# Moving the attention mask multiplication from VectorE to GpSimd and adding weight loads of the identity on TensorE

## What is computed

```python
q = k = v = src.reshape(B, S, H, 64).transpose(0, 2, 1, 3)
scores = q @ k.T                                # no scaling
valid  = (|k_pos - q_pos| <= 256) & inside the sequence
attn   = softmax(where(valid, scores, -1e9)) @ v
x  = layernorm(src + attn)
x  = layernorm(x + relu(x @ W1 + b1) @ W2 + b2)     # 1024 -> 4096 -> 1024
x  = layernorm(src + x)
x  = layernorm(x + moe(x))     # 8 experts, the top 2 weighted by a gate, silu(gate) * up
```

## Time and profile before

| | us |
|---|---|
| runs of the kernel | 3070.01 and 3357.81, median 3213.91 |
| the profiled execution | 3068.48, its span 3067.3 (cores 3056.1 to 3067.3) |
| attention | 481 of the span |
| TensorE busy, whole span | 2279.9 (74%) |
| VectorE busy, whole span | 942.5 (31%) |
| ScalarE busy, whole span | 507.6 (17%) |
| GpSimd busy, whole span | 147.5 (5%), issues of DMAs and four small fills at the start |

### The profile page before, as it was taken

The page is one execution under the profiler, slowest core; times in us unless marked ns, Lnnn a source line. Parts: engine busy times, 40 slices in busy tenths (PEclk is TensorE's granted clock), DMA queues, the critical chain, the costliest instruction groups (busy, mean ns, idle before and its releaser), DMA issues.

```text
span 3067.3 us, 30932 instructions; the slowest of 8 cores (3056.1 to 3067.3 us)
## 1 busy us (share of the span) xinstructions
PE 2279.9 (74%) x11113; PEld 1085.0 (35%) x11290; DVE 942.5 (31%) x1837; ACT 507.6 (17%) x750; POOL 147.5 (5%) x282
## 2 busy tenths in 40 slices
PE   0487777522998899303299988999899988999863
PEld 0244444311444344102144434444344443444431
DVE  0244455465000500554333311332123321233133
ACT  0233343200310220000011111111111111111110
POOL 2000000000000000000000010000100001000000
PEclk9999999999999899755599999999999999999987
DMA  9300000100443243030022233222332223322342
GB/s 220 73 1 1 1 1 1 42 0 0 72 79 69 48 78 67 14 110 0 21 35 42 42 62 58 40 43 47 58 60 35 43 48 62 55 42 38 52 97 75
DMA packets 49812, 148.14 MB, mean 48 GB/s; under 512 B 4936, under 2 KB 7664, under 8 KB 47616
## 3 DMA queue, kind: packets, MB, share of 16 engines
q0 software_dynamic: 39808, 115.49, 21.9%
q1 hardware_dynamic: 9856, 30.66, 3.3%
HBM read 248.96 MB, written 8.42 MB: 84 GB/s over the span
## 4 chain that ended last, share of the span: by engine, by line
PE 71%; DVE 12%; issue 5%; ACT 5%; DMA 4%; SPq 3%; DVEq 0%; ACTq 0%; POOL 0%; POOLq 0%
PE ob L652 14%; PE hg L587 14%; PE hu L587 14%; PE hb L467 7%; PE hb L438 7%; PE ps L331 5%; PE ppv L273 5%; DVE x0s L129 4%; DVE bn L129 3%; SPq L147 3%; ACT osb L139 2%; ACT strb L139 2%; DVE attnh L132 1%; PE ptm L293 1%; PE pbf L670 1%
## 5 line engine op out<-in xcount | busy, mean ns | idle before, releaser
L587 PE MATMUL hg<-ubf,w1T 128*128 128x512 bf16 x2007 | 482.9, 381 | 19.9 <-DMA w1T<-w1tt 10.1
L587 PE MATMUL hu<-ubf,w1T 128*128 128x512 bf16 x2007 | 479.9, 379 | 2.2
L652 PE MATMUL ob<-a,w2t 128*128 128x512 bf16 x1997 | 451.7, 381 | 17.3 <-DVE a L129 9.1
L129 DVE TENSOR_TENSOR x0s<-pbf,x0s 128x1024 f32<-128x1024 bf16 x80 | 97.9, 1224 | 928.2 <-PE pbf L670 493.6
L587 PEld LDWEIGHTS hg<-ubf,w1T 128*128 128x128 bf16 x2048 | 200.5, 98 | 261.6 <-issue 23.5
L129 DVE TENSOR_TENSOR sg<-sg,crep 128x512 bf16<-128x512 bf16 x256 | 108.8, 425 | 596.8 <-ACT sg L139 575.1
L587 PEld LDWEIGHTS hu<-ubf,w1T 128*128 128x128 bf16 x2048 | 200.5, 98 | 242.0 <-issue 0.7
L652 PEld LDWEIGHTS ob<-a,w2t 128*128 128x128 bf16 x2048 | 198.6, 98 | 246.0 <-issue 21.9
L139 ACT ACTIVATE sg<-hg 128x512 bf16<-128x512 f32 x256 | 152.9, 597 | 742.0 <-PE hu L587 742.0
L438 PE MATMUL hb<-ybf,w1buf 128*128 128x512 bf16 x1003 | 226.8, 386 | 14.7 <-ACT hsb L139 12.8
L139 ACT ACTIVATE strb<-ps 128x640 bf16<-128x640 f32 (+4 forms) x320 | 187.3, 597 | 288.4 <-PE ps L331 288.4
(11 more groups left out here) (64 smaller groups left out, 941.1 us busy)
## 6 DMA issues: line engine op xcount, KB each, us to landing
w1T<-w1tt POOLq DMA_DIRECT2D x64, 512.0 KB, 5.0
w2t<-w2tt POOLq DMA_DIRECT2D x128, 256.0 KB, 4.6
w1buf<-W1p POOLq DMA_DIRECT2D x32, 512.0 KB, 5.2
w2buf<-W2p POOLq DMA_DIRECT2D x16, 1024.0 KB, 9.0
x0s<-x SPq DMA_DIRECT2D x1, 8192.0 KB, 51.8
x0r<-x SPq DMA_DIRECT2D x1, 8192.0 KB, 28.1
out<-x0s SPq DMA_DIRECT2D x2, 4096.0 KB, 17.3
x0tm<-x0p POOLq DMA_DIRECT2D x20, 260.0 KB, 39.9
```

The source lines that it names most:

```text
L129: return self.vmark(getattr(self.nc.vector, name)(*args, **kw))
L587: ins = nc.tensor.matmul(hps[:], bass.AP(self.w1T, slot2 * 2048 + kc * 256 + hu * 128, [[2 * 2048, 128], [1, 128]]), self.ubf[:, kc, 512 * ...
L652: ins = nc.tensor.matmul(obp[:, 512 * nb:512 * nb + 512], self.w2t[:, dsl, eidx, 128 * jc:128 * jc + 128], self.a[:, eidx, jc, 1024 * half ...
```

## The change

The multiplication with the mask is issued on GpSimd in place of VectorE, with a semaphore of its own (`sGP`) that the products on TensorE, the reuse of the ring's slots by ScalarE, and the barriers wait for. Behind the scores of each strip one weight load of the 128x128 bf16 identity is issued on TensorE, and behind each group of five products two of them; no matmul uses these weights, since the next matmul is preceded by its own load. That is 320 + 2 x 256 = 832 weight loads more on a core.

```diff
--- before.py
+++ after.py
@@ -79,6 +79,8 @@
         self.sT = sem("sT")
         self.sV = sem("sV")
         self.sS = sem("sS")
+        self.sGP = sem("sGP")
+        self.cGP = 0
         self.NGL = 20
         self.NQL = 8
         self.gsems = [sem(f"g{i}") for i in range(self.NGL)]
@@ -138,6 +140,11 @@
     def sop_nw(self, name, *args, **kw):
         return self.smark(getattr(self.nc.scalar, name)(*args, **kw))
 
+    def gop_nw(self, name, *args, **kw):
+        self.cGP += 1
+        getattr(self.nc.gpsimd, name)(*args, **kw).then_inc(self.sGP, 1)
+        return self.cGP
+
     def qdma(self, out, in_):
         i = self.qrr
         self.qrr = (self.qrr + 1) % self.NQL
@@ -180,6 +187,7 @@
             self.wait(e, self.sT, self.cT)
             self.wait(e, self.sV, self.cV)
             self.wait(e, self.sS, self.cS)
+            self.wait(e, self.sGP, self.cGP)
             for i in range(self.NQL):
                 self.wait(e, self.qsems[i], self.qcnt[i])
             for i in range(self.NGL):
@@ -262,7 +270,7 @@
             grp = T // 4
             tloc = T % 4
             gb = h * 4 + grp
-            self.wait("tensor", self.sV, mask_mark[h * KT + T + 4])
+            self.wait("tensor", self.sGP, mask_mark[h * KT + T + 4])
             ppv = self.ppv[grp % 2]
             if tloc == 0:
                 self.wait("tensor", self.sV, evac_mark.get(gb - 2, 0))
@@ -275,6 +283,8 @@
                     self.x0tm[:, mm, 65 * h:65 * h + 65],
                     self.strb[:, sl, qc:qc + 128],
                     start=(i == 0), stop=(i == 4))
+            nc.tensor.ldweights(self.idb[:])
+            nc.tensor.ldweights(self.idb[:])
             pv_mark[gb] = pvm = self.tmark(ins)
             for mm in range(T, T + 5):
                 k = h * KT + mm
@@ -334,16 +344,18 @@
                         start=True, stop=True)
                     c0 += n
                 qk_m = self.tmark(ins)
+                nc.tensor.ldweights(self.idb[:])
                 self.wait("scalar", self.sT, qk_m)
                 if gidx >= RING:
                     self.wait("scalar", self.sT, strip_last_pv.get(gidx - RING, 0))
+                    self.wait("scalar", self.sGP, mask_mark.get(gidx - RING, 0))
                 exp_mark[gidx] = self.sop_nw(
                     "activation", self.strb[:, slot, 0:w], ps[:, 0:w],
                     AF.Exp, bias=-SHIFT, scale=1.0)
-                self.wait("vector", self.sS, exp_mark[gidx])
+                self.wait("gpsimd", self.sS, exp_mark[gidx])
                 if gidx >= RING:
-                    self.wait("vector", self.sT, strip_last_pv.get(gidx - RING, 0))
-                mask_mark[gidx] = self.vop_nw(
+                    self.wait("gpsimd", self.sT, strip_last_pv.get(gidx - RING, 0))
+                mask_mark[gidx] = self.gop_nw(
                     "tensor_mul", self.strb[:, slot, 0:w],
                     self.strb[:, slot, 0:w], self.msk[:, m, 0:w])
                 T = m - LAG
```

## The result

| | before | after |
|---|---|---|
| median of all runs (12 and 13) | 3107.43 us | 3111.56 us |
| ratio, after to before | | 1.007, 95% interval 1.0043 to 1.0097 |
| the profiled execution, its span | 3067.3 us | 3088.7 us |
| attention, every core | 481.7 us (481.4 to 481.8) | 497.2 us |

The account below looks back on a forecast made before the run. The prediction took TensorE in the attention, at 1.2 GHz and waiting for the copy at turns, as the bound. A head's +2.1 - 1.48 + 0.76 = +1.4 us gave +22 us on 3068.5, so 3090 us, range 3025 to 3140.

Parts of the forecast that it names:

- the sum: Attention, per head: +2.1 - 1.48 + 0.76 = +1.4 us; over 16 heads +22 us, attention 503 us.
- the same: Whole kernel: a change within about 2% (61 us), which a measurement cannot tell from no change; chance 0.72.
- In the other groups the mask hides behind TensorE: Groups after a head's first: GpSimd's masks cost nothing there, up to a price of about 1.6 us.
- The three steps behind the first products: Start of a head: products wait for masks 1.53 us apart instead of 1.31, 3 x 0.22 = 0.66 us more.
- Part 1: Turns inside a head: without the mask ahead on VectorE, the copy to attnh starts earlier, gaining 1.48 us a head.
- Part 2: GpSimd: a mask of 640 columns costs 1.53 us, 2.4 ns a column all in; bounds 0.77 and 2.06 us.
- Where the price lies: Start of a head: first products 1.44 us later, 2.1 us in all to the first turn; otherwise hidden behind TensorE.
- Part 3: TensorE in attention: 832 weight loads at 0.027 us each, 0.081 us a strip where TensorE sets the pace, 0.76 us a head.
- GpSimd setting the pace: Attention: a full strip's mask of 1.8 us or more makes GpSimd the bound, +62 us, from 3131 us; chance 0.17.
- Nothing moves: Attention: a cheap mask under 1.2 us with the clock unchanged gives 3045 to 3070 us; chance 0.05.
- The clock: TensorE in attention rises to the upper clock: 3020 to 3075 us, chance 0.20; with a cheap mask under 3007, chance 0.06.

Follow-up runs that it names:

- pool_only: The kernel after without its 832 weight loads, so only the mask moves to GpSimd; attention 492.3 us, +10.6 against the kernel before.
- order: The kernel before with the newest strip's mask issued on VectorE behind the copy to attnh at the three turns inside a head; attention 458.5 us, ratio 0.9926.
- filler_all: order plus unread matmuls of 128x248 columns, two behind every group of products and four in each turn; attention 418 to 429 us.
- defer_fill2: order with each turn's transposes behind the next strip's scores, plus two unread 128x248 matmuls behind every group of products; attention 490 to 494 us, ratio 1.0048.
- loads_only: The kernel before with the 832 weight loads added, the mask staying on VectorE; attention 492.0 us, +10.3.
- loads8: The kernel before with eight weight loads of the identity behind each strip's scores, none behind the products; attention 579.0 us, +97.
- defer_fill1: order with each turn's transposes behind the next strip's scores, plus one unread 128x248 matmul behind every group of products; attention 441 to 444 us, ratio 0.9881.

## Why the prediction was right or wrong

- **The time, and against what.** The forecast was 3090 us, and the profiled execution of the kernel after took 3090.1 us, its span 3088.7. As a change from the profiled execution before, from which the prediction counted, it was +22 us, +0.7%, and the ratio says +0.7%. That the two agree so well is partly luck: the sum put all 22 us into the attention and nothing into the other stages, and the attention became longer by 15.5. Read against the median that stood beside it, 3213.91 us, 3090 us is a fall of 124 us, and no such fall came: the median of two runs 288 us apart was no time of this kernel (with twelve runs it is 3107.43 us), and the forecast should have named the change as a ratio. The prediction also took 2% (61 us) for what a measurement can tell, and gave "the same" 0.72; this step failed. The interval is 0.3% to either side, so the kernel is measurably slower, and the forecast's own +0.7% should have made "slower, by less than 2%" the statement.
- **The steps of the sum that failed** are an overlap and two sizes. "In the other groups the mask hides behind TensorE, up to a price of about 1.6 us" was put at nothing and measured 0.68 us a head in pool_only, at 1.39 us a mask. The three steps behind the first products were put at +0.66 us and measured +0.11. The weight loads were put at 0.76 us a head and measured 0.31 on top of the mask's move. The first two errors cancel: for the move alone the sum had 2.1 - 1.48 = +0.62 us a head, and pool_only has +0.69. That is luck.
- **Part 1, the copy behind the mask:** right. 1.48 us a head were forecast; order gives 29.94 - 28.48 = 1.46 us, and attention falls by 23.2 us where 16 x 1.48 is 23.7.
- **Part 2, the price of a mask:** 1.53 us taken, 1.39 us measured, 0.18 us fixed and 1.89 ns a column. The Trainium skill (GPSIMD Engine Reference, section 3.1) gives 2.6 cycles a column, 1.39 us by estimate, and the trace agrees for 640 columns; for 128 it would be 0.28 us, and the trace has 0.43, which the fixed part explains. The page was nearer than my row of VectorE's, and its advice (section 4.1) to keep elementwise work on VectorE held: pool_only is 10.6 us slower in the attention.
- **Where the price lies:** the first products were forecast 5.7 us behind the scores and are at 5.69 in the sixth head (5.74 in the mean). This is luck again: narrow masks were dearer and wide ones cheaper than I took them, and the first five come to 4.55 us where I had 4.59. The three steps behind, forecast at 1.53 us, take 1.35 to 1.37. The step before the third turn takes 1.38 us and not 1.10, because with narrower scores TensorE's own step (1.21, 1.10) is shorter than a mask of 640 columns; I looked at the wide steps only.
- **Part 3, the weight loads:** forecast 0.027 us each, 0.76 us a head. Alone they cost 10.3 / 16 = 0.64 us; one of three costs 0.05 and the others nothing. On top of GpSimd's pace they cost 4.9 / 16 = 0.31 us a head, since GpSimd and no longer TensorE sets most steps. The price from the gate's row did not carry over: a load behind another load costs 0.047 us, and one behind a matmul that covers it nothing.
- **The sum:** +1.38 us a head forecast, +1.00 measured, +22 against +15.5 us in the attention.
- **The rivals.** GpSimd setting the pace: in part, from a price of 1.35 us a strip on, since steps of 1.31 are already under it, but far from the point (1.8 us) at which it decides. "Nothing moves" needed a mask under 1.2 us, and it takes 1.39. The clock: it stayed down, and eight loads a strip did not lift it. The rule of the Trainium skill (TensorE: Matmul & The Clock Gate, Part 1), that the slow level is the default and sustained activity lifts it, agrees with filler_all (mean clock 0.81) but not with defer_fill2, where TensorE was busy for 280.03 of 290 us at 0.50; here the measurement decides. The weight loads of loads_only and loads8 left matmuls of 512 columns at 598 and 603 ns.

## What to carry to other kernels

A wait of the bottleneck for an engine that is half idle can be the order on that engine's queue and not its load, as it was here for 23 us. Before moving work to another engine, see what stands right ahead of the instruction that is waited for, and move that behind it (order gained 23 us, where the engine's change cost 10.6). Then ask what the waiting engine could do meanwhile: issuing the next scores ahead of the transposes brought another 44 us. When an engine takes over a chain of small operations, compare its price with the shortest steps of the bottleneck and with the first ones after a restart, not with the mean.

## What the runs showed of the hardware that I had not expected

- GpSimd's product of two bf16 tiles costs 0.18 us + 1.89 ns a column (0.43 us for 128, 1.39 us for 640 columns), 2.8 times VectorE's 0.49 us at 640.
- A weight load of 128x128 bf16 at the lower clock costs nothing behind a matmul that covers it, 0.05 us behind the scores, 0.047 us apiece in a row of eight; in the gate, with matmuls of 8 columns between, 0.027 us.
- Attention matmuls, busy for 79% of the stage, ran at 1.2 GHz throughout while the clock column read 1.00. Two extra full-array matmuls of 248 columns behind each group and four in each turn brought TensorE to 2.4 GHz for 62% of the time (filler_all) and made the stage shorter by 29 to 40 us than order, although they are wasted work.
- A TensorE almost without gaps is not enough for the upper clock: in defer_fill2 it was busy for 280.03 of 290 us at a granted clock of 0.50. And before the first recorded change the clock column reads 1.00 even at the lower clock (defer_fill1: 1.00 with 512-column matmuls at 602 ns up to 197 us, then 0.56).
